# Five one-value-per-row steps of a feed-forward pipeline moved from the vector engine to GpSimd

## The reference, cut to what matters

```
x = x + ffn(layernorm(x))                     # mean and variance over 512, eps 1e-5
def ffn(x):
    h = silu(bit_linear(x, w_gate)) * bit_linear(x, w_up)          # [tokens, 2048]
    h = ln_weight * (h * rsqrt(mean(h * h) + 1e-6))                # rms norm
    return bit_linear(h, w_down)                                   # [tokens, 512]
def bit_linear(x, w):      # activations to 8 bits by the row's largest magnitude
    s = 127 / clip(max(abs(x)), 1e-5)
    return (clip(round(x * s), -128, 127) / s) @ ternary(w).T
```

## Time and profile before

| | us |
|---|---|
| median of 3 runs (lowest, highest) | 786.46 (786.30, 791.66) |
| the profiled execution, its own time | 788.57 |
| its span, first to last instruction | 786.80 |
| feed-forward, from the hidden of quarter 3 of tile 0 to that of tile 15 | 165.82 |
| PE busy, all of the span | 731.5 (93%) |
| DVE busy | 595.6 (76%) |
| ACT busy | 471.6 (60%) |
| POOL busy | 332.3 (42%) |

### The profile page before, as it was taken

One profiled execution on the slowest core, in us unless ns is written; L12 is line 12 of the kernel. 1 busy time (PEld: TensorE's weight loads), 2 busy tenths in 40 slices (PEclk: granted clock), 3 DMA queues, 4 the chain that ended last, 5 costly groups with the idle time before them and its releaser, 6 DMA issues. The chain is left out here.

```text
span 786.8 us, 14092 instructions
## 1 busy us (share of the span) xinstructions
PE 731.5 (93%) x5113; PEld 506.2 (64%) x5130; DVE 595.6 (76%) x1103; ACT 471.6 (60%) x1024; POOL 332.3 (42%) x329
## 2 busy tenths in 40 slices
PE   5988999999999999999987969999998999999993
PEld 4865777777777777777765657888874444444441
DVE  6886766885667866766677547887888999999993
ACT  4555666766676666666665314444455777677761
POOL 2011205213242134254464344445546667787661
PEclk9998999999999999999999979999999999999998
DMA  9300013214131322314311065555431233243322
GB/s 310 119 1 27 28 33 103 69 68 141 50 99 37 108 84 78 108 55 148 139 65 55 1 227 225 177 193 199 155 114 37 53 82 94 81 108 94 81 73 61
DMA packets 55218, 78.33 MB, mean 100 GB/s; under 512 B 36335, under 2 KB 38383, under 8 KB 53424
## 3 DMA queue, kind: packets, MB, share of 16 engines
q1 hardware_dynamic: 46336, 51.99, 20.9%
q0 software_dynamic: 8528, 24.93, 9.3%
q10 hardware_dynamic: 288, 0.52, 0.2%
HBM read 56.92 MB, written 17.59 MB: 95 GB/s over the span
## 5 line engine op out<-in xcount | busy, mean ns | idle before, releaser
L556 ACT ACTIVATE probs<-s_ps,neg_max 128x512 f32<-128x512 f32 (+2 forms) x256 | 152.5, 611 | 19.4 <-DVE neg_max L725 17.6
L725 DVE TENSOR_REDUCE neg_max<-s_ps 128x2 f32<-128x1024 f32 (+2 forms) x128 | 124.6, 1015 | 36.0 <-PE s_ps L963 35.6
L983 PE MATMUL pT_ps<-ident,probs 128*128 128x128 f32 x832 | 114.7, 279 | 9.6 <-DVE probs L746 8.6
L568 ACT ACTIVATE probs<-pT_ps 128x512 f32<-128x512 f32 x96 | 57.5, 599 | 98.4 <-PE pT_ps L983 97.6
L983 PEld LDWEIGHTS pT_ps<-ident,probs 128*128 128x128 f32 x832 | 93.4, 143 | 24.8 <-DVE probs L746 11.3
L746 DVE COPY probs<-pT_ps 128x512 f32<-128x512 f32 x112 | 76.8, 686 | 36.4 <-PE pT_ps L983 36.4
L1682 POOL TENSOR_TENSOR xg_own<-h,ln_w_sb 128x512 f32<-128x512 f32 x63 | 82.7, 1323 | 33.3 <-DVE h L1771 33.2
L896 PE MATMUL side_ps<-w_hi 128*128 128x512 f32 x172 | 71.1, 413 | 0.0
L420 POOL TENSOR_TENSOR aT_hi<-norm,one_col 128x512 fp32r<-128x512 f32 x15 | 15.6, 1040 | 124.8 <-DVE norm L737 86.6
L896 PE MATMUL side_ps<-w_hi,w_lo 128*128 128x512 f32 x172 | 67.5, 392 | 0.0
L896 PE MATMUL side_ps<-w_lo,w_hi 128*128 128x512 f32 x172 | 67.0, 389 | 0.0
(11 more groups left out here) (289 smaller groups left out, 1775.7 us busy)
## 6 DMA issues: line engine op xcount, KB each, us to landing
w_piece<-w_ffn SPq DMA_DIRECT2D x24, 512.0 KB, 3.6
w_stage<-w_ffn SPq DMA_DIRECT2D x12, 1024.0 KB, 4.9
xres<-x POOLq DMA_DIRECT2D x4, 1024.0 KB, 5.6
xn<-x SPq DMA_DIRECT2D x3, 1024.0 KB
x<-xres POOLq DMA_DIRECT2D x3, 1024.0 KB, 4.8
xn<-c SPq DMA_DIRECT2D x2, 1024.0 KB, 5.9
v_next<-c SPq DMA_DIRECT2D x2, 1024.0 KB, 7.6
xn<-x SPq DMA_DIRECT2D x4, 256.0 KB, 3.6
```

Source lines behind the costliest of these rows:

```text
L556: nc.scalar.activation(weights[qt][:, h, at:at + width(qt)], s_ps[:, h, 0:width(qt)], ACT.Exp, bias=neg_max[:, qt % 2, h:h + 1], accum_out ...
L568: nc.scalar.activation(out, turned_p, ACT.Identity).then_inc(slot_copied[0], 1)
L725: nc.vector.tensor_reduce(neg_max[:, qt % 2, 2 * s:2 * s + 2], s_ps[:, 2 * s:2 * s + 2, 0:width(qt)], AX.X, ALU.max, negate=True).then_inc ...
L983: last = nc.tensor.transpose(pT_ps[:, k % 2, h * P:h * P + P], weights[qt][:, h, a:z], ident[:])
```

## The change

The five steps are issued by POOL in place of DVE. POOL gets the two steps on the sum of squares ahead of the power for h_rms, variance plus epsilon ahead of the power for rstd, the mean step behind it, and y_scale of tile t-1 between weighted quarter 3 and gu_scale. Each step that reads the one before it waits for its semaphore, also on the same engine. New waits across engines: DVE's variance waits until the mean of two tiles before is done, h_max waits until y_scale of the tile before has read it, the result waits for its y_scale, and POOL's h_rms waits until DVE has used the old one.

```diff
-XQ_STEPS, HQ_STEPS = 3, 5
+XQ_STEPS, HQ_STEPS = 3, 4
     def rstd_of(self, pool, t):
         i = t % 2
+        pool.wait_ge(self.stats_done, t + 1)
+        self.nc.gpsimd.tensor_scalar(self.var_eps[:, i:i + 1], self.bn_mv[:, i, 1:2], LN_EPS, None, ALU.add).then_inc(self.eps_added, 1)
         pool.wait_ge(self.eps_added, t + 1)
...
             .then_inc(self.rstd_ready, 1)
+        pool.wait_ge(self.rstd_ready, t + 1)
+        self.nc.gpsimd.tensor_scalar(self.mean_rstd[:, i:i + 1], self.bn_mv[:, i, 0:1], self.rstd[:, i:i + 1], -1.0,
+                                     ALU.mult, ALU.mult).then_inc(self.mean_ready, 1)
...
     def variance_of(self, dve, t):
         dve.wait_ge(self.stats_step, t + 1)
+        if t >= 2:
+            dve.wait_ge(self.mean_ready, t - 1)
         self.nc.vector.bn_aggr(self.bn_mv[:, i, :], self.bn_st[:, i, :]).then_inc(self.stats_done, 1)
-        dve.wait_ge(self.stats_done, t + 1)
-        self.nc.vector.tensor_scalar(self.var_eps[:, i:i + 1], self.bn_mv[:, i, 1:2], LN_EPS, None, ALU.add).then_inc(self.eps_added, 1)
-
-    def mean_of(self, dve, t):
...
         def rms_of(t):
-            pool.wait_ge(h_var_ready, t + 1)
+            pool.wait_ge(sq_ready, (t + 1) * HALVES)
+            nc.gpsimd.tensor_tensor(h_ss[:], h_sq[:, t % 2, 0:1], h_sq[:, t % 2, 1:2], ALU.add).then_inc(rms_step, 1)
+            pool.wait_ge(rms_step, 2 * t + 1)
+            nc.gpsimd.tensor_scalar(h_var[:], h_ss[:], 1.0 / F, RMS_EPS, ALU.mult, ALU.add).then_inc(rms_step, 1)
+            pool.wait_ge(rms_step, 2 * t + 2)
+            if inside(t - 1):
+                pool.wait_ge(hq_step, t * HQ_STEPS)
             nc.gpsimd.tensor_tensor(h_rms[:], h_var[:], minus_half[:], ALU.pow).then_inc(rms_ready, 1)
+
+        def y_scale_of(t):
+            n = t % (LATE_DOWN + 2)
+            pool.wait_ge(hq_step, t * HQ_STEPS + 2)
+            if t >= LATE_DOWN + 2:
+                pool.wait_ge(y_ready, t - LATE_DOWN - 1)
+            nc.gpsimd.tensor_scalar(y_scale[:, n:n + 1], h_max[:], w_mean[:, 2:3], 1.0 / QMAX, ALU.mult, ALU.mult)\
+                .then_inc(y_scale_ready, 1)
...
             if t < TILES - 1:
                 weighted(t, 3)
+            if inside(t - 1):
+                y_scale_of(t - 1)
             if inside(t + 2):
                 front.gu_scale_of(pool, t + 2)
...
-        def sum_squares(t):
-            dve.wait_ge(sq_ready, (t + 1) * HALVES)
...
             dve.wait_ge(rms_ready, t + 1)
+            if inside(t - 1):
+                dve.wait_ge(y_scale_ready, t)
             nc.vector.tensor_scalar(h_max[:], h_top[:], h_rms[:], Q_EPS, ALU.mult, ALU.max).then_inc(hq_step, 1)
```

More of the change, by code:

```diff
@@ L1487, in vector_program @@
                 front.variance_of(dve, 1)
-            if s == last - 2:
-                front.mean_of(dve, 0)
-                front.mean_of(dve, 1)
             if s == last - 1:
@@ L1616, in ffn_phase @@
     hw_last_ready = sem("hw_last_ready")
-    ss_ready, h_var_ready, rms_ready = sem("ss_ready"), sem("h_var_ready"), sem("rms_ready")
+    rms_step, rms_ready, y_scale_ready = sem("rms_step"), sem("rms_ready"), sem("y_scale_ready")
     hq_step, hq_ready = sem("hq_step"), sem("hq_ready")
@@ L1709, in gpsimd_program @@
         rms_of(TILES - 1)
+        y_scale_of(TILES - 1)
         for t in range(TILES - LATE_DOWN - 1, TILES):
@@ L1788, in top_of @@
                                     apply_absolute_value=True).then_inc(hw_max_ready, 1)
-        def sum_squares(t):
-            dve.wait_ge(sq_ready, (t + 1) * HALVES)
-            nc.vector.tensor_reduce(h_ss[:], h_sq[:, t % 2, :], AX.X, ALU.add).then_inc(ss_ready, 1)
-            dve.wait_ge(ss_ready, t + 1)
-            nc.vector.tensor_scalar(h_var[:], h_ss[:], 1.0 / F, RMS_EPS, ALU.mult, ALU.add).then_inc(h_var_ready, 1)
         def scale_h(t):
@@ L1805, in scale_h @@
             nc.vector.reciprocal(h_inv[:], h_max[:]).then_inc(hq_step, 1)
-            nc.vector.tensor_scalar(y_scale[:, t % (LATE_DOWN + 2):t % (LATE_DOWN + 2) + 1], h_max[:], w_mean[:, 2:3], 1.0 / QMAX, ALU.mult, ALU.mult)\
-                .then_inc(hq_step, 1)
-            dve.wait_ge(hq_step, at + 4)
+            dve.wait_ge(hq_step, at + 3)
             nc.vector.tensor_scalar(h_mul[:], h_inv[:], h_rms[:], QMAX, ALU.mult, ALU.mult).then_inc(hq_step, 1)
@@ L1822, in y_of @@
             dve.wait_ge(y_summed, t + 1)
+            dve.wait_ge(y_scale_ready, t + 1)
             nc.vector.scalar_tensor_tensor(xt[t], sums_of(t), y_scale[:, t % (LATE_DOWN + 2):t % (LATE_DOWN + 2) + 1], xt[t],
@@ L1826, in vector_program @@
         for t in range(TILES):
-            if inside(t + 2):
-                front.mean_of(dve, t + 2)
             if inside(t - 1):
@@ L1860, in vector_program @@
         top_of(last, 1)
-        sum_squares(last)
         scale_h(last)
```

2 lines of the change are left out of this document (removed).

## The result

The changed kernel takes 799.32 us (median of 6 runs, 798.26 to 801.76) where the kernel before takes 787.35 (6 runs beside it): ratio 1.0147, 95% interval 1.0121 to 1.0173. It is 12.0 us slower; forecast were 6. The two profiled executions differ by less, 796.6 - 786.8 = 9.8 us of span. Both medians are within 1.3 us of their profiled execution (798.36 and 788.57), on opposite sides, which makes the 2.2 between 9.8 and 12.0. What follows splits the 9.8.

The account below looks back on a forecast made before the run. POOL's in-order loop was taken to bound the eight gather cycles: 12.12 us against 11.22 costs 7.2, other cycles win 1.2, so +6.0 on the median of 786.46 gives 792.5 us; 8-in-10 range 784.5 to 801.0.

Parts of the forecast that it names:

- +7.2 - 1.2 = +6.0: Whole kernel: eight gather cycles lose 7.2 us, the other cycles win 1.2, start and end count 0.
- rival A: POOL's steps cost more than its multiply suggests: 801 us at the upper end, 798.3 at twice DVE's price; chance 0.25.
- The bound: Gather cycles: POOL's in-order loop sets the 11.22 us; part of DVE's 10.83 busy us is waiting for POOL.
- The size of the gather cycles: POOL's loop of 10.88 us plus 1.24 for the new steps gives 12.12 against 11.22, 0.90 more per gather cycle.
- 1.24: Price of the five steps on POOL per cycle: two of 0.20 us and three of 0.28 with a wait.
- Rival B: Gather cycles: the steps fall into POOL's waits and DVE's relief counts, ending at PE's 10.87; 781.6 us, chance 0.07.
- rival C: Nothing changes: the loop has play, gather cycles lose only what the others win; 786.5 us within 1, chance 0.08.
- slower by over 1%: Whole kernel above 794.3 us: A and a quarter of the forecast's chance, given 0.40.
- The turn of the order: Gather cycles: the first quantizing half asks before weighted quarter 1 and goes between quarters 0 and 1, taking 0.55 us.
- the turn changes the packs' time but not this sum: Gather cycles: with halves behind both quarters, the same 2.49 and 1.10 us would stand in POOL's loop in another order.
- PE leaves ... 2.1 at most: Cycles without gather: PE leaves 0.62 us in cycle 1, 0.35 or 0.23 in others, 2.1 in all; 1.2 was taken.
- PE's down product of the tile before is late at the same place, so I count 0: Behind the last tile: h_max waits 0.70 us for h_rms and POOL starts that chain earlier, yet no gain is counted.

Follow-up runs that it names:

- the relieved: The kernel before with DVE's five steps left out and nothing put on POOL in their place: 785.92 us, ratio 0.9977.
- the loaded kernel: The kernel before with five more steps of the same forms on POOL, results unread, and nothing taken from DVE: 803.66 us, ratio 1.0191.
- the shifted list: The changed kernel with 120 waits on a counter long reached ahead of PE's expert-stage work, 60 more PE instructions: 801.74 us, ratio 1.0171.
- the three with added waits: 120 PE waits added to the changed kernel (801.74 us), the kernel before (792.57), and the one with three steps on POOL and early store (785.32).
- the fastest kernel: The changed kernel with epsilon and mean back on DVE and the store moved between weighted quarters 1 and 2: 782.55 us, ratio 0.9936.

## Why the prediction was right and wrong

**What failed.** The mechanism held; the sum "+7.2 - 1.2 = +6.0" was too small. The profiled executions differ by 9.8: 1.5 more than foretold in the gather cycles (8.7 for 7.2, where the five steps, the store and the power behind epsilon were priced too low), 0.5 less won in the other cycles (0.7 for 1.2), 1.5 lost at the end and 0.2 at the start, both counted as 0. The other 2.2 of the 12.0 lie between the medians and these executions and are put down to no step. The time of 799.32 lies outside the forecast's 789 to 796 and beside the 798.3 of rival A, but not by A's mechanism: its cycle of 12.82 and its steps of 1.94 were 12.37 and 1.34. That the whole came out near A's is chance; the lost end and the distance between executions filled it up.

**The bound: right.** The in-order loop on POOL through the gather cycles, with DVE's full-looking 10.83 behind it, is what the relieved and the loaded kernel show: 11.22 and 12.37.

**The size of the gather cycles: too small by a quarter of a microsecond.** Foretold were 12.12, measured 12.37. Term by term, the stretch from quarter 0 to epsilon was foretold at 5.74 and took 5.76, gather, power and gu_scale were right within 0.02. The steps were priced too low: y_scale 0.22, sum 0.29, scaling 0.27, epsilon 0.33, mean 0.23 make 1.34 where "1.24" stood, and the power's 0.63 was 0.67. The store took 1.43, not 1.36. With 7 cycles of 1.14 and a first of 0.74 that is 8.72, not 7.2. Rival B, DVE's relief counting in these cycles, and rival C fell with the relieved and the loaded kernel. Rival A with 0.30 and more a step was too dear, and "slower by over 1%", which was given 0.40, is where the time fell.

The Trainium skill (GPSIMD Engine Reference, Engine selection) has two-input elementwise work about twice as slow on POOL. Of the five steps only the sum has two tensors as inputs: 0.29 by the starts above, the next step's wait for it counted in, against 0.15 for DVE's reduce; that is near the rule, for another operation on DVE. The prediction's 798.3 put all five under that rule; together they take 1.34 against 2 x 0.20 + 3 x 0.15 = 0.85 by the durations on DVE, 1.6 times. Its rule of timing by starts (Perfetto Trace Analysis, GPSIMD Engine Instruction) agrees: y_scale is recorded at 0.27, and gu_scale starts after 0.22.

**The turn of the order: half right.** The half did go between the quarters, as foretold. That "the turn changes the packs' time but not this sum" was wrong by 0.22 in its favour. It did not spoil the sum, which was made for the turned order and set against a measured 11.22.

**The other cycles: too hopeful.** 0.69 won, not 1.2. The step "PE leaves ... 2.1 at most" was wrong in kind, since DVE's relief alone wins 3.74 there. What eats it is POOL's load, 2.73 alone, which the prediction charged to the gather cycles only. In cycles 0 to 3 the undone kernels show both sides: with sum and scaling back on DVE they take 45.28 in place of 43.25, with epsilon and mean back 41.38.

**The start and the end: the end was not nothing.** At the start +0.23. The step "PE's down product of the tile before is late at the same place, so I count 0" looked at the right place and took the lateness as fixed. In the kernel before it is a landing of 3.9 us beside a code packet, and the packet moved to the first half: +1.54, of which the shifted list gives back 1.38. That the packet holds the transposes is shown by moving it.

The packet comes 1.6 us earlier against the first transposes. 1.0 of that is the transposes: the packs of tile 14 come that much later against the last hidden (771.95 to 774.29 against 762.67 to 766.03 us). Here the order turned the other way, which the prediction did not look for. POOL and DVE, kernel before, then changed kernel:

```profile
760.83 2.94 POOL L1682 TENSOR_TENSOR xg_own<-h,ln_w_sb 128x512 f32<-128x512 f32 x2
761.77 2.55 DVE L1818 TENSOR_SCALAR hq_big<-xg_own,h_mul 128x1024 f32<-128x1024 f32 x2
```

```profile
768.88 2.49 POOL L1692 TENSOR_TENSOR xg_own<-h,ln_w_sb 128x512 f32<-128x512 f32 x2
770.25 2.33 DVE L1825 TENSOR_SCALAR hq_big<-xg_own,h_mul 128x1024 f32<-128x1024 f32 x2
```

Before, the first half went between the quarters (2.94); now it asks 0.12 after quarter 0's end by the 1.25 of its kind, and comes behind quarter 1 (2.49). In every kernel with sum and scaling on DVE the first transposes are issued 2.2 us ahead of the last hidden, in every other 1.2. The other 0.6 is the packet, 0.66 behind the last hidden before and 0.06 now. It goes with epsilon and mean: the packet comes 0.06 to 0.08 behind it in all kernels with these two steps moved to POOL, 0.6 and more in the others but for the 0.3 of the load alone (leaving out the three with added waits). Why is open; PE's list is the same in both kernels.

## What to carry to other kernels

A busy share of 75% can be a full engine: follow the engine's list in order, from one instruction to the same one a round later, and see whether any wait lies where the new work would stand. The same instruction costs little inside a wait and its full price outside it: the store takes 1.43 of POOL's list, and putting it into the wait bought back 1.10 us a cycle, nearly all that the five steps cost (1.15), though the time then only came level with the kernel before. And before work is moved off an engine, relieve it on trial with the work left out: in the gather cycles, where the change was to pay, that was worth nothing (89.77 us against 89.82).

## What the runs showed of the hardware

One 16 KB packet of the instruction queue held up transposing DMAs in flight: single packets of theirs took up to 2.3 us in place of 0.02, and the transposes landed after up to 4.9 us in place of 2.7. Which transfer it meets hangs on the length of an engine's list, so an edit far away, or on another engine, can shift it. The queue q8 is PE's by the shift: counted from the end of PE's recorded list (with its weight loads), its last packet comes with 96 to 103 instructions to go in the eleven kernels without the added waits, and with 156 to 158 in the three with them.

PE's busy time in a stretch is not a floor: a gather cycle has 10.87 busy, and the fastest kernel does the same 53 recorded products in a cycle of 10.77. The profile models the ends of matmuls; which of them it has too late is not shown.

PE's granted clock fell from 1.00 to 0.50 (1.2 GHz) within 1.3 us of the end of PE's wait for the transposes in five kernels, which waited 2.35 to 3.04 us, and came back after 3.4 or 6.8 us. It did not fall there with waits of 2.35 and 2.48 us in two others, so this wait alone does not decide it.

A quantizing half that asks while POOL runs a weighted quarter waits for that quarter's end, and then sometimes lets the next quarter pass. How early it asks does not settle which. In the kernel with sum and scaling back DVE's half starts at 663.38, 0.34 before the end of quarter 0 by the 1.25 of its kind, and both halves come after quarter 1; in the changed kernel it starts at 663.54, 0.45 before that end, and goes first; in the kernel before, in cycle 13, it starts 0.31 before that end and goes first too. The two orders differ by 0.22 a gather cycle; what decides was not tried.
